# Attention with a hand-written order of queues: the output's turn placed between the third and fourth block of weight turns, and VectorE's block move placed ahead of the output add

## The reference, cut to what matters

```python
x = x + _L0_gnn_ref(_layernorm(x), batch0, edge_index, L0_gnn_W)
x = x + _L0_ffn_ref(_layernorm(x)[None], ...)[0]
x = x + _L1_gnn_ref(_layernorm(x), ...)
x = x + _L1_ffn_ref(_layernorm(x)[None], ...)[0]
```

```python
aw = jnp.einsum('ehf,ehf->eh', q[src], k[dest])
e = jnp.exp(aw - m[src])
alpha = e / denom[src]
out = jax.ops.segment_sum(alpha[:, :, None] * v[dest], src, num_segments=n)
```

## Time and profile before

| | us |
|---|---|
| median of 3 runs | 900.56 |
| lowest and highest of them | 898.99, 901.5 |
| the profiled execution, first to last instruction | 898.3 |
| TensorE busy in it | 846.5 |
| VectorE busy in it | 567.0 |
| ScalarE busy in it | 374.2 |
| GpSimd busy in it | 206.3 |
| attention loop, first output's turn to the last value product of unit 39 | 208.0 to 507.9 |

### The profile page before, as it was taken

The page is one execution under the profiler, slowest core; times in us unless marked ns, Lnnn a source line. Parts: engine busy times, 40 slices in busy tenths (PEclk is TensorE's granted clock), DMA queues, the critical chain, the costliest instruction groups (busy, mean ns, idle before and its releaser), DMA issues.

```text
span 898.3 us, 16248 instructions
## 1 busy us (share of the span) xinstructions
PE 846.5 (94%) x5209; PEld 575.8 (64%) x5209; DVE 567.0 (63%) x1878; ACT 374.2 (42%) x680; POOL 206.3 (23%) x379
## 2 busy tenths in 40 slices
PE   6999998989999999999999899999988999996996
PEld 3456555447777777777777677777674445675664
DVE  6489999446777888788778365555534414875111
ACT  1234443446665566666556433334310012543331
POOL 4100000000021022012103241212236511465453
PEclk9999999999999999999999999999999999996998
DMA  9818988888101313111643827455135360175550
GB/s 261 319 28 200 209 215 204 130 303 212 34 26 30 106 54 95 42 53 25 230 128 106 262 67 214 155 178 160 60 92 128 82 197 12 35 244 129 166 172 24
DMA packets 87365, 121.02 MB, mean 135 GB/s; under 512 B 40782, under 2 KB 50158, under 8 KB 87022
## 3 DMA queue, kind: packets, MB, share of 16 engines
q1 hardware_dynamic: 73677, 101.82, 39.8%
q0 software_dynamic: 13600, 18.11, 7.3%
HBM read 65.52 MB, written 57.08 MB: 136 GB/s over the span
## 4 chain that ended last, share of the span: by engine, by line
PE 75%; DVE 12%; DMA 5%; issue 3%; ACT 2%; POOL 1%; SPq 1%; DVEq 0%; POOLq 0%; ACTq 0%
PE ps L787 17%; PE ps L678 10%; PE ps L707 10%; PE ps L917 9%; PE ps L689 8%; PE ps L568 5%; PE ps L944 4%; PE ps L794 4%; DVE R_B L1811 4%; DVE R_B L1810 2%; PE ps L573 2%; DMA R_A<-slots_d 1%; DVE R_A L1912 1%; PE ps L518 1%; DVE R_B L1806 1%
## 5 line engine op out<-in xcount | busy, mean ns | idle before, releaser
L787 PE MATMUL ps<-R_B,R_A 128*128 x612 | 184.6, 444 | 1.7 <-ACT R_A L1281 0.6
L787 PEld LDWEIGHTS ps<-R_B,R_A 128*128 128x128 f32 x612 | 111.2, 193 | 34.6 <-issue 24.5
L1217 ACT ACTIVATE R_A<-R_A,neg_max 125x1250 f32<-125x1250 f32 x80 | 106.6, 1333 | 58.2 <-DVE neg_max L1912 58.2
L1912 DVE CUSTOM_DVE_ANT_0 R_A<-ps,R_B,neg_max 125x417 f32<-125x417 f32 (+1 forms) x160 | 97.6, 648 | 29.1 <-PE ps L678 29.1
L678 PE MATMUL ps<-R_B 64*125 64x417 f32 (+1 forms) x480 | 106.5, 544 | 3.1 <-DVE neg_max L1912 1.6
L707 PEld LDWEIGHTS ps<-R_W,XN 125*64 125x64 f32 x1600 | 85.3, 136 | 23.1 <-issue 23.0
L689 PE MATMUL ps<-ident,R_A 125*125 125x125 f32 x800 | 98.7, 278 | 0.0
L689 PEld LDWEIGHTS ps<-ident,R_A 125*125 125x125 f32 x800 | 94.9, 188 | 1.5 <-DVE R_W L1919 0.7
L707 PE MATMUL ps<-R_W,XN 125*64 125x125 f32 x1600 | 94.7, 272 | 0.0
L1224 ACT ACTIVATE R_W<-ps 125x500 f32<-125x500 f32 x120 | 66.1, 585 | 51.3 <-PE ps L689 51.3
L1811 DVE TENSOR_SCALAR R_B<-R_B 125x418 bf16<-125x418 uint16 x200 | 77.2, 386 | 0.0
(11 more groups left out here) (269 smaller groups left out, 1178.0 us busy)
## 6 DMA issues: line engine op xcount, KB each, us to landing
slots_d<-R_B SPq DMA_DIRECT2D x9, 2322.0 KB, 12.4
R_B<-in_L_ffn_w_dram SPq DMA_DIRECT2D x28, 512.0 KB, 7.4
R_A<-slots_d SPq DMA_DIRECT2D x27, 256.0 KB, 2.8
slots_d<-R_A SPq DMA_DIRECT2D x27, 256.0 KB, 2.6
counts_d<-R_A SPq DMA_DIRECT2D x10, 546.9 KB
logs_d<-R_B SPq DMA_DIRECT2D x10, 546.9 KB
R_B<-logs_d SPq DMA_DIRECT2D x10, 546.9 KB
R_B<-counts_d SPq DMA_DIRECT2D x10, 546.9 KB
```

Of the source, the lines that this page charges most:

```text
L787: ins = pe.matmul(bank(b, TM, width), lhs[:, c * TM:c * TM + TM], flat[:, bass.ds(e * (n * width) + c * width, width)], start=c == 0, stop ...
L1217: act.activation(SC[u % 2][h], SC[u % 2][h], ACT.Exp, bias=neg_max[:, 2 * (u % 2) + h:2 * (u % 2) + h + 1], scale=-1.0, accum_out=den[:, 2 ...
L1912: dve.tensor_tensor_reduce(SC[u % 2][h][:, a:z], bank(2 * h + g % 2, P, z - a), LNB[i % 2][:, a:z], -1.0, least if t else 3.0e38, ALU.add, ...
```

## The change

`turn_weights` takes the blocks that it is to turn. TensorE turns blocks 0 to 2, then the output of u-2, then blocks 3 and 4. VectorE moves block 2 directly after the two thirds of `negate_scores`, ahead of `add_output`, of the copies of logits or ranks, and of the row statistics.

```diff
@@ block.tensor
-            def turn_weights(u):
+            def turn_weights(u, blocks):
 
-                for b in range(BLOCKS):
+                for b in blocks:
                     n = ring_at(u, b)
                     release_ring(n - 3)
                     for k in range(4):
@@ block.tensor, the loop over the units
                     rank_tile(tile_at(u, RANKS_AT))
                     if tile_at(u, RANKS_AT) == EARLY_ROWS:
                         take_out_counts(EARLY_ROWS % 2)
+                turn_weights(u, range(0, 3))
                 if 2 <= u:
                     turn_output(u - 2)
-                turn_weights(u)
+                turn_weights(u, range(3, BLOCKS))
                 if tile_at(u, ROWS_AT) is not None:
                     turn_normed_row(tile_at(u, ROWS_AT))
@@ block.vector, the loop over the units
                     negate_scores(u + 1, 0)
                     negate_scores(u + 1, 1)
+                move_block(u, DVE_BLOCKS[0])
                 if 2 <= u:
                     add_output(u - 2)
                 if tile_at(u, LOGITS_AT) is not None:
                     take_logits(tile_at(u, LOGITS_AT))
                 if tile_at(u, RANKS_AT) is not None:
                     take_ranks(tile_at(u, RANKS_AT))
                 if tile_at(u, STATS_AT) is not None:
                     dve.wait_ge(S("x_added"), 2 * (u - 1))
                     row_stats(X, tile_at(u, STATS_AT))
-                move_block(u, DVE_BLOCKS[0])
                 inverse_den(u)
```

## The result

The changed kernel takes 895.5 us, median of ten runs (894.73 to 899.26), against 901.14 for the kernel before in as many (898.99 to 904.85): a ratio of 0.9947, with an interval of 0.9929 to 0.9964. The forecast was 899.4, in a range of 897.4 to 902.2, and no change that can be told from scatter. The profiled span went from 898.3 to 893.0 us.

The account below looks back on a forecast made before the run. TensorE was taken as the bound, busy 846.5 of 898.3 us. The terms -1.9 - 0.35 + 0.8 + 0.25 = -1.2 us, off the median of 900.56, gave 899.4, range 897.4 to 902.2.

Parts of the forecast that it names:

- The output's turn between two squares: TensorE's run of twenty squares: the output's turn costs 0.02 us more there than in front, 38 times, 0.8 us lost.
- if its load hides wholly: Output's turn in its new place: lower bound, 0.10 us less each, 3.8 us gained over 38; given 0.02.
- The move in the row turn: Block 2's move ahead of the add on VectorE: removes a 0.24 us TensorE stall in eight row turns, 1.9 us gained.
- TensorE's arrival: Row turn: TensorE reaches the normed row at 428.95 or a little later, 2.59 us after 426.36.
- u = 38: Ninth row turn, VectorE late from the mixture's bookkeeping: 0.35 us gained, 0.47 of stall left after the add's 0.39.
- The last unit: u = 39, with no next scores to hide behind: values wait for the later add, 0.25 us lost.
- The values' wait for the add: Value products in u = 39: the add ends later and the logits are visible about 500.9, so 0.25 us lost.
- VectorE's first move there: Sign in the row turns: a first weight move on VectorE that waits for TensorE would make the prediction wrong.
- statistics, logits and ranks stayed covered: Later VectorE steps in the loop cost 0: cover of 1.0 us for statistics, 0.6 in logits turns, rank turns alike.
- the queues: DMA and engine queues: no moved step issues a DMA, no SyncE load stands behind one; no loss.
- the seam: Row tile 3's load after the loop: rival, up to 3.6 us gained or as much lost; chance 0.12, 0.08 for better.
- The signs that were set down: Changed profile: plain turn 7.41 us against 7.39, output's turn 0.12 from neighbouring squares, L734's wait gone in eight row turns.

## Why the prediction was wrong

**The step that failed** is "The output's turn between two squares". It took the price from an average, 2.38 us for twenty squares, and the average held two waits (0.11 us) and the longer step to the next scores (0.09). The pace of the squares is 0.109 us, and the run with the output's turn inside takes 223.41 - 220.92 = 2.49 us to the next scores, from the timeline of u = 4 after:

```profile
220.92 1.38 PEld L689 LDWEIGHTS ps<-ident,R_A 125*125 125x125 f32 x12 [0.60 <-issue]
...
222.23 0.19 PEld L716 LDWEIGHTS ps<-ident,R_W 128*125 128x125 f32 x1
...
222.34 0.95 PEld L689 LDWEIGHTS ps<-ident,R_A 125*125 125x125 f32 x8
...
223.41 0.29 PEld L678 LDWEIGHTS ps<-R_B 64*125 64x125 f32 x4
```

That is what the unit without an output's turn needed before, 2.49. I read this row as the price of the instruction, 0.10, and it was, but for another reason than I thought: with twenty squares the two waits stood bare in either case. I wrote 38 x 0.02 = 0.8 us lost; it was 3.1 gained in the loop (291.83 with the move alone, less 288.72), nearly all of it in the 28 turns that are not row turns. The result lies near the end of my bounds, 3.8 gained "if its load hides wholly", to which I gave 0.02 since I had no mechanism for it. The list of waits has next to nothing of it: before, waits of squares for ScalarE stand in it once, with 0.2 us in all, because the trace's matmuls overlap and a wait of 0.05 to 0.07 us leaves no idle time between them.

I weighed the Trainium skill here (TensorE: Matmul & The Clock Gate, "LDWEIGHTS (loading the stationary operand)"), whose figure comes to 104 ns, as an estimate, for 125 columns, and let the trace decide against it with 0.119. The measured pace is 0.109, so the page was nearer, and the difference between 0.119 and it was the sign that I missed. The Trainium skill (Perfetto Trace Analysis, "Optimization Strategy") also says that the same gap coming back on the engine that should be saturated can mean too few buffers. The trace agrees in that 0.11 us a turn comes back at the first reuse of two of the three banks; no run here adds a bank.

**The move in the row turn** was right in kind, short in size: 0.24 a turn predicted, 0.386 measured with the ring's share in it. Alone the move gave 8.196 - 7.828 = 0.368. VectorE's times were right: I had the row ready to start 428.80 - 426.36 = 2.44 us after the start of the run of squares, and in u = 30 after it starts 2.44 after it (422.445 - 420.005). TensorE's arrival was wrong. I took 2.59, which is the arrival of the next scores, waits included, and so counted only 0.24. The twenty squares and the output's turn start within 2.18 us after the change, and at one place of 0.109 the row could come at 2.29. VectorE is the later one, and the row gained what VectorE gained, 2.83 - 2.44 = 0.39.

**u = 38** gained 0.29 (0.35 predicted). The wait is left, in the timeline after:

```profile
484.19 0.67 DVE L1920 COPY R_W<-ps 125x500 f32<-125x500 f32 x1
...
484.92 0.64 PE L734 MATMUL ps<-ident,R_B 125*128 125x125 f32 x4 [0.63 <-DVE R_W L1920]
```

**The last unit** lost some 0.47, not 0.25. The values' wait for the add came as forecast but longer, since the output's turn stands behind block 2 and the add behind the move: the values start 12.88 us after the start of turn 38, against 12.46 with the last unit as before, which is 0.42 of it. Another 0.04 lies at the ranks behind it, which I had left out; they wait for GpSimd there, 0.47 us, where they waited 0.42 for ScalarE before:

```profile
491.67 0.68 DVE L1920 COPY R_W<-ps 125x500 f32<-125x500 f32 x1 [2.93 <-PE ps L689]
492.27 0.47 DVE L1941 SCALAR_TENSOR_TENSOR X<-ps,rden,X 125x64 f32<-125x64 f32 x2
...
493.01 2.37 PE L707 MATMUL ps<-R_W,XN 125*64 125x125 f32 x40 [0.45 <-DVE X L1941]
...
495.85 0.36 PE L751 MATMUL ps<-counted,before 126*126 126x8 f32 x2 [0.47 <-POOL counted L1503]
```

**What held:** in the list of waits L734's went in eight row turns and stayed in the ninth, though by the starts some 0.1 us is left in each of the eight; VectorE's first move there does not wait for TensorE (it starts 421.720 - 420.005 = 1.72 us after the first load in u = 30, and block 2 is there after 1.62); L707 waits for the add nowhere but in the last unit; statistics, logits and ranks stayed covered, as did the queues; the seam moved by less than 0.1 us (153.25 and 153.34). **The signs that were set down** fell with the step: the plain turn came to 7.28, not 7.41, and the output's turn stands 0.109 from its neighbours, not 0.12. By the measured terms the sum is -6.09 in the loop and +0.16 behind it, -5.9; the medians moved by 5.64.

## What to carry to other kernels

Before an instruction is priced by the mean pace of a run, look at the spacing of the starts in it one by one: a place where the pace breaks can be a wait, even if no idle time is listed, and an independent instruction put exactly there was free here. In this ring of banks, which feeds slower movers, that place is at the first use of a bank that has to be emptied, and behind the blocks whose moves have to start early. A gain at the end of a loop is worth what the next stage's loads allow: here the step that releases those loads was moved back for it, and the 1.2 us gained came with a longer stage behind (157.04 in the one trace, 153.31 to 155.78 without it).

## What was not expected of the hardware

- A load of 125 columns with its product of 125 columns keeps a pace of 0.109 us; the granted clock was 1.00 (2.4 GHz) through the loop. Between the starts of the products, the first one after long score products takes 0.21 (222.82 to 223.03 before) and the way from the last square to the next score product 0.20; between the starts of the loads it is 0.106 and 0.31.
- ScalarE's move of a 125x500 block lasts 0.587 us, but a second one starts 0.48 us after the first (223.67 and 224.15), and TensorE's next load follows 0.05 after a move's end. In the changed kernel the 17th square still comes 0.05 after the end of the second move (222.78 and 222.73 in u = 4), so the free place is just filled.
- TensorE's waits of 0.05 and 0.07 us in the plain turns are not listed as idle time. The two together were worth 0.11 us a turn, 3.1 us of the kernel.
- The same kernel begins its loop anywhere between 191.4 and 197.5 us, and the stage after the loop varied by 2.5 us, while 38 turns of the loop repeat within 0.02 us. Why was not tried.
